# Turning q and k by transposing DMAs instead of TensorE in a streamed two-layer transformer kernel

## The chip, the cores and the metric

The kernel runs on one NeuronCore of one Trainium2 chip. The metric is the device time of one execution in microseconds (us).

## The reference, cut to what matters

The input is two sequences of 2048 tokens of 128 channels. A softmax self-attention comes first, then a two-layer local-attention transformer, then a token-weighting block, then the same two layers again (each behind a layer norm). The change lies wholly in the two-layer block:

```python
def local_attention(q, k, v):                  # 8 heads of 64, windows of 64 tokens
    bq, bk, bv = q.reshape(b, h, w, 64, d) * 8, k.reshape(b, h, w, 64, d), v.reshape(b, h, w, 64, d)
    bk, bv = look_around(bk), look_around(bv)  # the window before, and the own
    sim = einsum('bhwid,bhwjd->bhwij', bq, bk) # masked: i < j or i > j + 64
    return einsum('bhwij,bhwjd->bhwid', softmax(sim), bv)

def _layer(x, ...):
    q, k, v = split(shift_token(x) @ wqkv, 3)
    q, k = rotary_xpos(l2norm(q) * qs, l2norm(k) * ksc)
    x = x + local_attention(q, k, v) @ wo
    h = layernorm(shift_token(x)) @ w1 + b1
    a, g = split(h, 2)
    return x + (a * gelu(g)) @ w2 + b2
```

## The kernel before, in words

Values stay as high and low parts (a value rounded, and the rest), and a product is made of three products of parts (`halves`, L193 to L196). The two-layer block runs twice, as u = 0 and u = 1 (`layers_*`, stages 4 and 8). It streams 128-token tiles: 64 tiles per stage (TS), that is 32 of the first layer and 32 of the second, in STEPS = 68 steps. At step s each engine does its part for several tiles at once: tile s is projected, tile s-1 is normed and gets its rotary factors, tile s-2 is turned, tile s-3 gets its scores, tile s-4 is finished. The feed-forward works on chunks C of 512 tokens (four tiles), spread over the steps by `chunk_at(s, r)`, which is C where s = 4C + r. So the work repeats every four steps.

What each engine does in a step, in the order in which it is written (an engine takes its instructions in that order):

- PE (`layers_pe`): `scores(s-3)` (L647, banks 4 and 5) and `take_off_maxima(s-3)` (L670), `turn(s-2)` (L609: eight fp32 128x128 transposes at L615 from the token rows `ta` into PSUM banks 2 and 3), `turn_result(s-4)` (L696), `project(s)` (L598, q and k into banks 0 and 1), `feed_forward(s)` (L758), `project_out(s-4)` (L703, bank 5), `values(s-2)` (L620, bank 4), `maxima(s-2)` (L628, banks 2 and 3 again), `gather(s-3)` (L679, banks 6 and 7). In the step with `centred` (L738, bank 5) `values` goes ahead of `project_out`.
- ACT (`layers_act`): `exps(s-3)` (L871), `high(s-2)` (L852: the turned q and k out of PSUM, rounded to bf16 into the ring H; L860 copies 64 columns more at the ring's end), `copy_result(s-4)` (L877), `squares(s)` (L840), gates or `square` or `deviation` of the feed-forward, `copy_values(s-2)` (L863), `rnorms(s)` (L845), gelus with two loads of activation tables in every fourth step (L928, L958).
- DVE (`layers_dve`): `divide(s-4)` (L1071), `normed(s-1)` (L1031, which reads banks 0 and 1), `rope(s-1)` (L1040, times cosine into `ta`), `low(s-2)` (L1050: PSUM minus H into the ring L), `gated`, `add_out(s-4)` (L1081), `norms(s)` (L1026), `reduce_maxima(s-2)` (L1064), `scaled` (L1087).
- POOL (`layers_pool`): `rope(s-1)` (L1182: times sine at L1188, two additions into `ta` at L1194), `scale_tables` (L1175), and the low parts of the feed-forward and attention inputs.
- SP (`layers_sp`): issues the DMAs: `tables(s+2)` (L541), shifted inputs (L521), `own(s-2)` (L548) and `past(s-2)` (L555), which copy values across partitions.

Three waits order the neighbours of the change. `project(s)` waits for `normed(s-1)` (L603), as both use banks 0 and 1; `feed_forward(s)` waits for `copy_result(s-4)` (L759 and L760), as bank 7 is used by both; and DVE's `add_out(s-4)` waits for `project_out(s-4)` (L1084) and stands ahead of `norms(s)` and `reduce_maxima(s-2)`.

Of the kernel before, what the change touches and what calls it, by code (L numbers as in the profile page):

```python
# [50 lines left out]
def build(nc, a, out):  # L51
    ctx = ExitStack()
    with ctx:
        def sb(name, shape, dt=F32):
# [10 lines left out]
            "la_pj la_sq la_ss la_rn la_qn la_ta la_tc la_rp la_tr la_hi la_lo la_mx la_mr "  # L65
# [43 lines left out]
        with x_scope:  # L109
# [22 lines left out]
            with ExitStack() as sc:  # L132
                BL = Names(sq=arena(sc, [NH * 2, DH]), qn=arena(sc, [NH * 2, DH]),
                           ta=[arena(sc, [NH * 2, DH]) for _ in range(2)], tc=arena(sc, [NH * 2, DH]),
                           ss=arena(sc, [2, 32]), H=arena(sc, [2, 4, RQ * 128 + 64], BF16),
                           L=arena(sc, [2, 4, RQ * 128 + 64], BF16), mx=[arena(sc, [8], BF16) for _ in range(2)],
                           va=[arena(sc, [NH, DH + 1]) for _ in range(2)], vs=[arena(sc, [NH, DH + 1]) for _ in range(2)],
                           PT=[arena(sc, [2, 512]) for _ in range(2)], rc=[arena(sc, [2, 4, 1]) for _ in range(2)],
                           o=[arena(sc, [2, 4, DH]) for _ in range(2)], ot=[arena(sc, [4, 128]) for _ in range(2)],
                           tb=[arena(sc, [4 * DH]) for _ in range(4)], ysl=arena(sc, [CH]), ysf=arena(sc, [CH]),  # L140
                           hf=[arena(sc, [CH]) for _ in range(2)])
# [374 lines left out]

        def layers_sp(e, stage, u, k):
# [44 lines left out]

            tables(0)
# [4 lines left out]
            for s in range(STEPS):  # L568
                if s + 2 < TS:
                    tables(s + 2)  # L570
                if chunk_at(s, -3):
                    shift_for_attention(chunk_at(s, -3))
                if chunk_at(s, 7) is not None:
                    shift_for_feed_forward(chunk_at(s, 7))
                if 0 <= s - 2 < TS:
                    own(s - 2)
                    past(s - 2)

        def layers_pe(e, stage, u):
# [29 lines left out]
            def turn(i):  # L609
                e.wait_ge(S.la_mr, hi(i))  # L610
                e.wait_ge(S.la_rp, 2 * hi(i) + 2)
                e.wait_ge(S.w_bb, 1)
                for x in range(2):
                    for j in range(4):
                        mm = e.e.transpose(PS[:, 2 + x, j * 128:(j + 1) * 128],  # L615
                                           BL.ta[i % 2][:, 8 * x + 2 * j:8 * x + 2 * j + 2, :].rearrange("p a b -> p (a b)"),
                                           ident)
                mm.then_inc(S.la_tr, 1)
# [84 lines left out]
            def project_out(i):  # L703
# [4 lines left out]
                if chunk_at(i + 4, 9) is not None:  # L708
                    e.wait_ge(S.ff_sq, NC * u + chunk_at(i + 4, 9) + 1)
# [28 lines left out]
            def centred(C):  # L738
                e.wait_ge(S.sf_lo, NC * u + C + 1)
                e.wait_ge(S.la_e, hi(min(4 * C + 6, TS - 1)) + 1)  # L740
                e.e.matmul(PS[:, 5, :], cenr[:, :], fed(HH, C), start=True, stop=False)
                e.e.matmul(PS[:, 5, :], cenr[:, :], fed(HL, C), start=False, stop=True).then_inc(S.ff_cen, 1)
# [15 lines left out]
            def feed_forward(s):  # L758
# [12 lines left out]
                if chunk_at(s, 9) is not None:  # L771
                    centred(chunk_at(s, 9))
# [5 lines left out]
            for s in range(STEPS):  # L778
# [36 lines left out]
            centred(Z)  # L815
# [15 lines left out]
        def layers_act(e, stage, u):  # L831
# [20 lines left out]
            def high(i):  # L852
                c0 = (i % RQ) * 128
                src = PS[:, 2:4, :].rearrange("p x (c q) -> p x c q", q=128)
                e.wait_ge(S.la_tr, hi(i) + 1)
                if i >= RQ - 1:
                    e.wait_ge(S.la_s, hi(i - RQ + 1) + 1)
                o = e.e.copy(BL.H[:, :, :, 64 + c0:192 + c0], src)  # L858
                if i % RQ == RQ - 1 and i % NT < NT - 1:
                    o = e.e.copy(BL.H[:, 1, :, 0:64], src[:, 1, :, 64:128])  # L860
                o.then_inc(S.la_hi, 1)

            def copy_values(i):  # L863
# [5 lines left out]
                e.e.copy(BL.va[i % 2][:, :, 0:DH], PS[:, 4, :].rearrange("p (h d) -> p h d", d=DH)).then_inc(S.la_va, 1)  # L869
# [27 lines left out]
            def square(C):  # L897
# [3 lines left out]
                e.e.activation(BF.sq, PS[:, 5, :], ACT.Square).then_inc(S.ff_sq, 1)  # L901
# [44 lines left out]
            for s in range(STEPS):  # L946
# [49 lines left out]
            square(Z)  # L996
# [11 lines left out]
        def layers_dve(e, stage, u):  # L1008
# [31 lines left out]
            def rope(i):  # L1040
                e.wait_ge(S.la_qn, hi(i) + 1)
                if i >= 2:
                    e.wait_ge(S.la_tr, hi(i - 2) + 1)
                e.wait_ge(S.tb_sc, hi(i) + 1)
                cos = BL.tb[i % 4].rearrange("p (c x o d) -> p c x o d", c=2, x=2, o=1)[:, 0]
                e.e.tensor_tensor(BL.ta[i % 2].rearrange("p (x h) d -> p x h d", x=2),  # L1046
# [69 lines left out]
            for s in range(STEPS):  # L1116
# [55 lines left out]
        def layers_pool(e, stage, u):  # L1172
# [9 lines left out]
            def rope(i):  # L1182
# [9 lines left out]
                tv = BL.ta[i % 2]  # L1192
# [493 lines left out]
```

## Time and profile before

| | us |
|---|---|
| median of 3 runs | 1744.61 (1741.96 to 1745.35) |
| the profiled execution, whole | 1745.16 |
| its span in the profile | 1743.4 |
| first two-layer stage | about 260 to 950 |
| second two-layer stage | about 1020 to 1715 |

| engine | busy | share |
|---|---|---|
| PE (matmul) | 1573.1 | 90% |
| DVE | 1294.5 | 74% |
| ACT | 1190.2 | 68% |
| POOL | 1180.5 | 68% |

The profile shows one execution. Matmuls are pipelined, so their busy times overlap and PE's share is not its share of peak. A chain of waits follows the work that ended last back through what released each piece; a piece's length in that chain is the time it adds, while the mean duration of an instruction in the groups may overlap its neighbours. "to landing" is the time from a DMA's issue to its completion.

### The profile page before, as it was taken

The numbers are of one execution on the slowest core, as the hardware profiler recorded it, in microseconds if no ns is written. First come the engines' busy times: TensorE is split into PE (matmuls) and PEld (weight loads), VectorE is DVE, ScalarE is ACT, GpSimd is POOL, SyncE is SP. The second block draws the span as 40 slices with busy tenths as digits, with TensorE's granted clock in tenths as the row PEclk, the third lists the DMA queues.
The fourth block names the chain that finished last, engine by engine and source line by source line (L and its number), as shares of the span: only waits on it lengthen the run. The fifth ranks groups of instructions, "written<-read, shape, count | busy, mean of one in ns | idle before, by whom it ended". The sixth has DMA issues, their size and how long they took to land.

```text
span 1743.4 us, 47775 instructions
## 1 busy us (share of the span) xinstructions
PE 1573.1 (90%) x20039; PEld 1235.7 (71%) x20039; DVE 1294.5 (74%) x1712; ACT 1190.2 (68%) x1848; POOL 1180.5 (68%) x778
## 2 busy tenths in 40 slices
PE   5999978999999999999986577999999999999986
PEld 4777846877777777777764455877777777777764
DVE  6776657888777877777755867888777877777763
ACT  4886854677766777777765764676776677767764
POOL 3010027888888788888861547888888878888860
PEclk8999988999999999999998887999999999999998
DMA  4000001222222222222110001222222222222111
GB/s 113 25 9 1 0 24 42 66 56 60 51 51 51 62 54 51 51 55 54 42 29 6 1 13 50 66 54 57 56 53 51 53 58 57 50 52 55 45 30 55
DMA packets 66145, 78.87 MB, mean 45 GB/s; under 512 B 14146, under 2 KB 41868, under 8 KB 65932
## 3 DMA queue, kind: packets, MB, share of 16 engines
q1 hardware_dynamic: 65932, 75.82, 17.9%
q8 instruction: 159, 2.61, 0.6%
q14 instruction: 54, 0.44, 0.1%
HBM read 23.10 MB, written 2.10 MB: 14 GB/s over the span
## 4 chain that ended last, share of the span: by engine, by line
PE 60%; ACT 16%; DVE 16%; issue 4%; POOL 2%; DMA 1%; DVEq 0%; POOLq 0%; SPq 0%; ACTq 0%
PE PS L194 9%; PE PS L196 8%; PE PS L195 8%; PE PS L711 7%; PE PS L692 4%; DVE t L1029 4%; PE PS L615 3%; PE PS L667 3%; PE PS L674 2%; ACT t L928 2%; DVE t L1035 2%; ACT L958 2%; ACT t L875 2%; ACT L928 2%; DVE t L1092 2%
## 5 line engine op out<-in xcount | busy, mean ns | idle before, releaser
L1188 POOL TENSOR_TENSOR t<-t 128x1024 f32<-128x1024 f32 x128 | 435.8, 3405 | 101.3 <-DVE t L1035 101.3
L1194 POOL TENSOR_TENSOR t<-t 128x512 f32<-128x512 f32 x256 | 322.1, 1280 | 18.6 <-POOL t L1188 0.4
L1085 DVE TENSOR_TENSOR yT<-PS,yT 128x128 f32<-128x128 f32 x128 | 37.3, 292 | 239.9 <-PE PS L711 239.6
L194 PE MATMUL PS<-wqh,HH 128*128 128x512 f32 x384 | 174.8, 455 | 29.5 <-DVE t L1035 17.9
L875 ACT ACTIVATE t<-PS 128x1024 f32<-128x1024 f32 x128 | 131.3, 1026 | 90.4 <-PE PS L674 89.9
L1212 POOL TENSOR_TENSOR HL<-t,HH 114x512 fp32r<-114x512 f32 (+1 forms) x84 | 118.2, 1421 | 103.9 <-ACT HH L942 103.9
L1046 DVE TENSOR_TENSOR t<-t 128x1024 f32<-128x1024 f32 x128 | 176.7, 1381 | 4.5
L843 ACT ACTIVATE t<-PS 128x1024 f32<-128x1024 f32 x128 | 131.3, 1026 | 71.3 <-PE PS L196 71.2
L1056 DVE TENSOR_TENSOR t<-PS,t 128x1024 bf16<-128x1024 f32 x128 | 155.9, 1218 | 20.7 <-ACT t L860 9.2
L1029 DVE TENSOR_REDUCE t<-t 128x16 f32<-128x1024 f32 x128 | 154.8, 1209 | 17.0 <-ACT t L843 16.7
L711 PEld LDWEIGHTS PS<-t,wo 128*128 128x128 f32 x1024 | 132.0, 192 | 35.4 <-issue 14.4
L1068 DVE TENSOR_REDUCE t<-PS 128x8 bf16<-128x1024 f32 x128 | 155.5, 1215 | 1.2 <-PE PS L641 1.2
L1035 DVE SCALAR_TENSOR_TENSOR t<-t,PS 128x1024 f32<-128x1024 f32 x128 | 154.7, 1209 | 1.9 <-ACT t L850 1.9
L196 PE MATMUL PS<-wqh,HL 128*128 128x512 f32 x384 | 154.9, 403 | 0.0
L195 PE MATMUL PS<-wql,HH 128*128 128x512 f32 x384 | 153.8, 400 | 0.0
L692 PE MATMUL PS<-t 128*64 128x65 f32 x4096 | 147.5, 224 | 0.0
L615 PE MATMUL PS<-cst,t 128*128 128x128 f32 x1024 | 135.5, 276 | 6.6 <-POOL t L1194 6.6
L711 PE MATMUL PS<-t,wo 128*128 128x128 f32 x1024 | 139.1, 279 | 0.4
L692 PEld LDWEIGHTS PS<-t 128*64 128x64 f32 x4096 | 129.8, 137 | 11.8
L858 ACT CAST t<-PS 128x1024 bf16<-128x1024 f32 x128 | 128.0, 1000 | 5.9 <-PE PS L615 5.8
L667 PEld LDWEIGHTS PS<-t 64*128 64x128 bf16 x6144 | 107.3, 95 | 14.3
L615 PEld LDWEIGHTS PS<-cst,t 128*128 128x128 f32 x1024 | 111.4, 142 | 8.3 <-POOL t L1194 8.3
(253 smaller groups left out, 3834.5 us busy)
## 6 DMA issues: line engine op xcount, KB each, us to landing
t<-t SPq DMA_DIRECT2D x254, 130.0 KB, 2.3
t<-in_c_rope SPq DMA_DIRECT2D x128, 128.0 KB, 2.8
t<-yT SPq DMA_DIRECT2D x112, 128.0 KB, 2.4
t<-in_L_attn_a_x SPq DMA_DIRECT2D x4, 512.0 KB, 7.1
out_x<-t SPq DMA_DIRECT2D x8, 256.0 KB, 3.6
t<-yT SPq DMA_DIRECT2D x16, 127.8 KB, 2.3
t<-in_L_ffn_wqkv SPq DMA_DIRECT2D x2, 768.0 KB, 4.2
t<-in_L_ffn_w SPq DMA_DIRECT2D x2, 341.0 KB, 3.3
```

The source lines that it names most:

```text
L194: e.matmul(o, ah, bh, start=not more, stop=False, skip_group_check=True)
L195: e.matmul(o, ah, bl, start=False, stop=False, skip_group_check=True)
L196: return e.matmul(o, al, bh, start=False, stop=stop, skip_group_check=True)
L615: mm = e.e.transpose(PS[:, 2 + x, j * 128:(j + 1) * 128], BL.ta[i % 2][:, 8 * x + 2 * j:8 * x + 2 * j + 2, :].rearrange("p a b -> p (a b)" ...
L692: mm = e.e.matmul(PS[rows[w], 6 + h // 4, 65 * (h % 4):65 * (h % 4) + 65], BL.PT[i % 2][:, h % 2, qs], V[:, h, :], start=True, stop=True, ...
L711: mm = e.e.matmul(PS[:, 5, 0:128], wo[:, l, j, :], BL.ot[i % 2][:, j, :], start=(j == 0), stop=(j == 3))
L875: e.e.activation(BL.PT[i % 2], PS[:, 4:6, :], ACT.Exp).then_inc(S.la_e, 1)
L1029: e.e.tensor_reduce(ss[:, 0:16], BL.sq, AX.X, ALU.add).then_inc(S.la_ss, 1)
L1035: e.e.scalar_tensor_tensor(BL.qn, ss[:, 16:32].rearrange("p (a o) -> p a o", o=1) .to_broadcast([128, 2 * NH, DH]), 1e12, PS[:, 0:2, :].re ...
L1046: e.e.tensor_tensor(BL.ta[i % 2].rearrange("p (x h) d -> p x h d", x=2), BL.qn.rearrange("p (x h) d -> p x h d", x=2), cos.to_broadcast([1 ...
L1188: e.e.tensor_tensor(BL.tc.rearrange("p (x h) d -> p x h d", x=2), BL.qn.rearrange("p (x h) d -> p x h d", x=2), sin.to_broadcast([128, 2, ...
L1194: e.e.tensor_tensor(tv[:, :, 32 * s:32 * s + 32], tv[:, :, 32 * s:32 * s + 32], BL.tc[:, :, 32 * (1 - s):32 * (1 - s) + 32], ALU.add).then ...
```

## The change

q and k no longer go through PSUM on their way to head-by-head layout. ACT's `high` rounds the token rows `ta` to bf16 (`qh`), DVE's `low` takes the rest as bf16 (`ql`), both from SBUF, and SP issues one transposing DMA of 128x1024 bf16 for each into the rings H and L, and a second, smaller one for each at the ring's end (every fourth tile, the last tile of a sequence apart). `ta` has one buffer in place of two. Banks 2 to 5 are dealt out anew: `values` uses bank 2 and stands ahead of `project`; `centred` uses bank 3. The semaphore la_tr goes, la_ht and la_lt come.

```diff
+        def turned(u, i):
+            return 16 * ((TS + TS // RQ - TS // NT) * u + i + i // RQ - i // NT)
...
 layers_sp
+            def turn(i, part, to, ready, sem):
+                c0 = (i % RQ) * 128
+                e.wait_ge(ready, hi(i) + 1)
+                if i >= RQ - 1:
+                    e.wait_ge(S.la_s, hi(i - RQ + 1) + 1)
+                e.wait_ge(sem, turned(u, i))
+                e.e.dma_start(to[:, :, :, 64 + c0:192 + c0].rearrange("p x c q -> p (x c) q"), part,
+                              transpose=True).then_inc(sem, 16)
+                if i % RQ == RQ - 1 and i % NT < NT - 1:
+                    e.e.dma_start(to[:, 1, :, 0:64], part[64:128, NH * DH:], transpose=True).then_inc(sem, 16)
...
                 if s + 2 < TS:
                     tables(s + 2)
+                if 0 <= s - 2 < TS:
+                    turn(s - 2, BL.qh, BL.H, S.la_hi, S.la_ht)
+                    own(s - 2)
+                    turn(s - 2, BL.ql, BL.L, S.la_lo, S.la_lt)
...
                 if 0 <= s - 2 < TS:
-                    own(s - 2)
                     past(s - 2)
...
 layers_pe
-            def turn(i):
-                e.wait_ge(S.la_mr, hi(i))
-                e.wait_ge(S.la_rp, 2 * hi(i) + 2)
-                e.wait_ge(S.w_bb, 1)
-                for x in range(2):
-                    for j in range(4):
-                        mm = e.e.transpose(PS[:, 2 + x, j * 128:(j + 1) * 128],
...
             def values(i):
-                e.wait_ge(S.la_e, hi(i))
+                e.wait_ge(S.la_mr, hi(i))
-                halves(e.e, PS[:, 4, :], h, hl, wqh[:, l, 1024:1536], wql[:, l, 1024:1536]).then_inc(S.la_v, 1)
+                halves(e.e, PS[:, 2, :], h, hl, wqh[:, l, 1024:1536], wql[:, l, 1024:1536]).then_inc(S.la_v, 1)
             def maxima(i):
-                e.wait_ge(S.la_hi, hi(i) + 1)
-                e.wait_ge(S.la_lo, hi(i) + 1)
+                e.wait_ge(S.la_ht, turned(u, i + 1))
+                e.wait_ge(S.la_lo, hi(i))
                 e.wait_ge(S.la_k0, u + 1)
+                e.wait_ge(S.la_va, hi(i) + 1)
+                e.wait_ge(S.w_bb, 1)
+                if chunk_at(i + 2, 9) is not None:
+                    e.wait_ge(S.ff_sq, NC * u + chunk_at(i + 2, 9) + 1)
             def scores(i):
-                e.wait_ge(S.la_va, hi(i) + 1)
+                e.wait_ge(S.la_e, hi(i))
                 e.wait_ge(S.la_out, hi(i - 1))
-                e.wait_ge(S.la_lo, hi(i) + 1)
+                e.wait_ge(S.la_lt, turned(u, i + 1))
             def centred(C, bank):
-                e.wait_ge(S.la_e, hi(min(4 * C + 6, TS - 1)) + 1)
+                e.wait_ge(S.la_mr, hi(min(4 * C + 6, TS - 1)) + 1)
...
                 if on(3):
                     scores(s - 3)
                     take_off_maxima(s - 3)
-                if on(2):
-                    turn(s - 2)
                 if on(4):
                     turn_result(s - 4)
+                if on(2):
+                    values(s - 2)
                 if on(0):
                     project(s)
                 feed_forward(s)
-                late = chunk_at(s, 9) is not None
-                if on(4) and not late:
-                    project_out(s - 4)
-                if on(2):
-                    values(s - 2)
-                if on(4) and late:
+                if on(4):
                     project_out(s - 4)
                 if on(2):
                     maxima(s - 2)
...
 layers_act
             def high(i):
+                e.wait_ge(S.la_rp, 2 * hi(i) + 2)
+                e.wait_ge(S.la_ht, turned(u, i))
+                e.wait_ge(S.la_lo, hi(i))
+                e.e.copy(BL.qh, BL.ta.rearrange("p a b -> p (a b)")).then_inc(S.la_hi, 1)
...
-                if on(3) and not after_gelus:
-                    exps(s - 3)
                 if on(2):
                     high(s - 2)
+                if after_gelus:
+                    e.e.preload_act_table_set("natural_log_exp_and_others")
+                if on(3):
+                    exps(s - 3)
                 if on(4):
                     copy_result(s - 4)
-                if after_gelus:
-                    e.e.preload_act_table_set("natural_log_exp_and_others")
-                if on(3) and after_gelus:
-                    exps(s - 3)
+                if on(2):
+                    copy_values(s - 2)
                 if on(0):
                     squares(s)
...
 layers_dve
             def rope(i):
                 e.wait_ge(S.la_qn, hi(i) + 1)
-                if i >= 2:
-                    e.wait_ge(S.la_tr, hi(i - 2) + 1)
+                e.wait_ge(S.la_lo, hi(i))
             def low(i):
                 e.wait_ge(S.la_hi, hi(i) + 1)
+                e.wait_ge(S.la_lt, turned(u, i))
+                o = e.e.tensor_tensor(BL.ql, BL.ta.rearrange("p a b -> p (a b)"), BL.qh, ALU.subtract)
...
                 if on(1):
                     normed(s - 1)
-                    rope(s - 1)
                 if on(2):
                     low(s - 2)
+                if on(1):
+                    rope(s - 1)
```

## Rows read from the trace of the kernel before

**Rows 1.** The page's part 1: busy us (share of the span) xinstructions.

```profile
PE 1573.1 (90%) x20039; PEld 1235.7 (71%) x20039; DVE 1294.5 (74%) x1712; ACT 1190.2 (68%) x1848; POOL 1180.5 (68%) x778
```

**Rows 2.** Windows: length, then busy us (xcount) by engine, PE clock, DMA share, GB/s.

```profile
300.00:900.00 600.00, 575.85 (x8759) 458.62 (x8757) 475.67 (x565) 426.71 (x666) 508.41 (x326) 1.00 0.22 53
900.00:960.00 60.00, 42.82 (x274) 28.93 (x274) 30.86 (x47) 33.82 (x52) 14.90 (x11) 0.86 0.03 7
```

**Rows 3.** The same view, one cycle of four steps, cut at `add_out`.

```profile
502.94:512.58 9.64, 9.18 (x146) 7.50 (x145) 8.15 (x10) 7.71 (x13) 9.50 (x7) 1.00 0.18 45
512.58:522.96 10.38, 10.38 (x152) 8.57 (x151) 6.93 (x9) 5.75 (x9) 9.94 (x7) 1.00 0.28 65
522.96:535.33 12.37, 11.09 (x154) 8.09 (x156) 9.31 (x12) 10.10 (x15) 8.88 (x7) 1.00 0.23 55
535.33:544.05 8.72, 8.70 (x142) 7.06 (x140) 7.92 (x10) 5.86 (x10) 5.98 (x4) 1.00 0.20 47
```

**Rows 4.** Chain of waits in that cycle, second step: start us, us, engine, line.

```profile
511.65 0.89 PE PS L711 x8
512.54 0.23 PE PS L194
...
513.24 0.34 PE PS L636 x4
...
513.80 1.08 PE PS L692 x32
...
516.46 0.88 PE PS L615 x8
...
517.77 0.23 PE PS L194
```

**Rows 5.** Timeline: start us, us, engine, line, operation, shapes, idle before it.

```profile
502.81 2.53 POOL L1194 TENSOR_TENSOR t<-t 128x512 f32<-128x512 f32 x2
...
507.34 1.21 DVE L1035 SCALAR_TENSOR_TENSOR t<-t,PS 128x1024 f32<-128x1024 f32 x1
...
512.58 0.29 DVE L1085 TENSOR_TENSOR yT<-PS,yT 128x128 f32<-128x128 f32 x1 [1.42 <-PE PS L711]
...
515.88 1.21 DVE L1035 SCALAR_TENSOR_TENSOR t<-t,PS 128x1024 f32<-128x1024 f32 x1
...
538.64 1.21 DVE L1035 SCALAR_TENSOR_TENSOR t<-t,PS 128x1024 f32<-128x1024 f32 x1
```

**Rows 6.** Chain of waits, third step: table load and exponentials.

```profile
530.28 1.28 ACT L958
531.58 1.03 ACT t L875
```

**Rows 7.** Groups of instructions: line, engine, operation, shapes | busy us, mean ns | idle before.

```profile
L1046 DVE TENSOR_TENSOR t<-t 128x1024 f32<-128x1024 f32 x128 | 176.7, 1381 | 4.5
L1056 DVE TENSOR_TENSOR t<-PS,t 128x1024 bf16<-128x1024 f32 x128 | 155.9, 1218 | 20.7 <-ACT t L860 9.2 <-ACT t L858 7.4
...
L858 ACT CAST t<-PS 128x1024 bf16<-128x1024 f32 x128 | 128.0, 1000 | 5.9 <-PE PS L615 5.8
...
L881 ACT COPY t<-PS 128x512 f32<-128x512 f32 x128 | 76.9, 600 | 1.9 <-PE PS L700 1.9
...
L860 ACT CAST t<-PS 128x256 bf16<-128x256 f32 x24 | 9.0, 375 | 0.0
```

**Rows 8.** DMA queues and issues: out<-in, KB each, median us to landing.

```profile
q1 hardware_dynamic: 65932, 75.82, 17.9%
...
t<-t SPq DMA_DIRECT2D x254, 130.0 KB, 2.3
...
t<-in_L_attn_a_x SPq DMA_DIRECT2D x4, 512.0 KB, 7.1
out_x<-t SPq DMA_DIRECT2D x8, 256.0 KB, 3.6
...
t<-cstv SPq DMA_DIRECT2D x16, 0.2 KB, 2.0
```

More of the change, by code:

```diff
@@ L64, in build @@
             "tb_ld tb_sc ys_l sl_hi sl_lo ys_f sf_hi sf_lo "
-            "la_pj la_sq la_ss la_rn la_qn la_ta la_tc la_rp la_tr la_hi la_lo la_mx la_mr "
+            "la_pj la_sq la_ss la_rn la_qn la_ta la_tc la_rp la_hi la_lo la_ht la_lt la_mx la_mr "
             "la_v la_va la_own la_past la_s la_e la_d la_rc la_ot la_ox la_oe la_po la_out la_k0 "
@@ L133, in build @@
                 BL = Names(sq=arena(sc, [NH * 2, DH]), qn=arena(sc, [NH * 2, DH]),
-                           ta=[arena(sc, [NH * 2, DH]) for _ in range(2)], tc=arena(sc, [NH * 2, DH]),
+                           ta=arena(sc, [NH * 2, DH]), qh=arena(sc, [2 * NH * DH], BF16), ql=arena(sc, [2 * NH * DH], BF16),
+                           tc=arena(sc, [NH * 2, DH]),
                            ss=arena(sc, [2, 32]), H=arena(sc, [2, 4, RQ * 128 + 64], BF16),
@@ L707, in project_out @@
                 e.wait_ge(S.la_out, hi(i))
-                if chunk_at(i + 4, 9) is not None:
-                    e.wait_ge(S.ff_sq, NC * u + chunk_at(i + 4, 9) + 1)
                 for j in range(4):
@@ L736, in first, with centred @@
                 halves(e.e, PS[0:CW[i], bank, :], w1h[:, l, cs], w1l[:, l, cs], fed(HH, C), fed(HL, C)).then_inc(sem, 1)
-            def centred(C):
+            def centred(C, bank):
                 e.wait_ge(S.sf_lo, NC * u + C + 1)
-                e.wait_ge(S.la_e, hi(min(4 * C + 6, TS - 1)) + 1)
-                e.e.matmul(PS[:, 5, :], cenr[:, :], fed(HH, C), start=True, stop=False)
-                e.e.matmul(PS[:, 5, :], cenr[:, :], fed(HL, C), start=False, stop=True).then_inc(S.ff_cen, 1)
+                e.wait_ge(S.la_mr, hi(min(4 * C + 6, TS - 1)) + 1)
+                e.e.matmul(PS[:, bank, :], cenr[:, :], fed(HH, C), start=True, stop=False)
+                e.e.matmul(PS[:, bank, :], cenr[:, :], fed(HL, C), start=False, stop=True).then_inc(S.ff_cen, 1)
             def variance(C, bank):
@@ L771, in feed_forward @@
                 if chunk_at(s, 9) is not None:
-                    centred(chunk_at(s, 9))
+                    centred(chunk_at(s, 9), 3)
                 if chunk_at(s, 14) is not None:
@@ L814, in layers_pe @@
             e.wait_ge(S.la_out, last)
-            centred(Z)
+            centred(Z, 5)
             e.wait_ge(S.la_e, last)
@@ L852, in high @@
             def high(i):
[L853 to L861, printed above, removed]
+                e.wait_ge(S.la_rp, 2 * hi(i) + 2)
+                e.wait_ge(S.la_ht, turned(u, i))
+                e.wait_ge(S.la_lo, hi(i))
+                e.e.copy(BL.qh, BL.ta.rearrange("p a b -> p (a b)")).then_inc(S.la_hi, 1)
             def copy_values(i):
@@ L868, in copy_values @@
                     e.wait_ge(S.la_past, 16 * (hi(i - 2) + 1 - u))
-                e.e.copy(BL.va[i % 2][:, :, 0:DH], PS[:, 4, :].rearrange("p (h d) -> p h d", d=DH)).then_inc(S.la_va, 1)
+                e.e.copy(BL.va[i % 2][:, :, 0:DH], PS[:, 2, :].rearrange("p (h d) -> p h d", d=DH)).then_inc(S.la_va, 1)
             def exps(i):
@@ L895, in high_for_feed_forward, with square @@
                 e.e.copy(fed(HH, C), BL.ysf).then_inc(S.sf_hi, 1)
-            def square(C):
+            def square(C, bank):
                 G = NC * u + C
@@ L900, in square @@
                 e.wait_ge(S.ff_var, G)
-                e.e.activation(BF.sq, PS[:, 5, :], ACT.Square).then_inc(S.ff_sq, 1)
+                e.e.activation(BF.sq, PS[:, bank, :], ACT.Square).then_inc(S.ff_sq, 1)
             def deviation(C, bank):
@@ L970, in layers_act @@
                 if chunk_at(s, 9) is not None:
-                    square(chunk_at(s, 9))
+                    square(chunk_at(s, 9), 3)
                 if chunk_at(s, 10) is not None:
                     deviation(chunk_at(s, 10), 7)
-                if on(2):
-                    copy_values(s - 2)
                 if on(0):
@@ L995, in layers_act @@
             high_hidden(B, 1)
-            square(Z)
+            square(Z, 5)
             high_hidden(B, 2)
@@ L1191, in rope @@
                 e.wait_ge(S.la_tc, g + 1)
-                tv = BL.ta[i % 2]
+                tv = BL.ta
                 for s in range(2):
```

13 lines of the change are left out of this document (2 added, 11 removed).

## The prediction

> **What bounds the kernel now.** I read the busy shares first: PE's 90% stands far above the rest [rows 1], and through the stream it is busy 576 of 600 us at the full clock, 2.4 GHz [rows 2]. That invites "less work on PE, less time". So I cut one four-step cycle into its steps at `add_out` [rows 3] and read the chain of waits and the timeline in it. I call the steps A, B, C, D: A is s mod 4 = 3, B is 0, C is 1, D is 2. Their lengths are 9.64, 10.38, 12.37 and 8.72 us, 41.1 together.
>
> From one `project_out` to the next `project` two paths run side by side. On PE, A to B: from 512.54 to 517.77 us, 5.23 us, with `turn` as 0.88 of it [rows 4]. On DVE: `add_out`, `norms`, `reduce_maxima`, `divide`, `normed`, from 512.58 to 515.88 + 1.21 = 517.09 us, 4.5 us [rows 5]; `project` may not start before. So PE is late by only about 0.6 us. From C to D `normed` ends at 538.64 + 1.21 = 539.85 us, 4.5 us after `add_out` at 535.33 [rows 3, 5], and `project` starts there at 539.9: a tie. From D to A DVE also has `scaled`, its `normed` ends at 508.55 us, 5.6 us after 502.94 [rows 3, 5], and PE waits for it. In C the chain leaves PE for ACT: gelus, `high`, L860, `copy_result`, table load, `exps` [rows 6, 7].
>
> **The change, part by part.**
>
> *PE's turning goes.* Eight transposes, 0.88 us of the chain in a tile [rows 4]; over 128 tiles 113 us, if PE were the bound everywhere. New PE path from `project_out` to `project`: 5.23 - 0.88 = 4.35 us (`values` has only moved inside it). DVE's path takes 4.5, and no edit shortens it. So the gain at A to B is what PE was late, about 0.4 us after the 0.1 us of handing over; at C to D none; at D to A none; at B to C none, as ACT's chain takes over there.
>
> *ACT in step C.* Before, from the end of `high` to `centred`: L860, `copy_result`, load, `exps`. ACT's instructions overlap by a tenth of a us, so in the chain high adds 0.9, L860 0.3, copy_result 0.5 and the load and exps 1.28 and 1.03 [rows 6, 7]: 4.0 us to 532.6, and 2.7 more to the step's end at 535.3 [rows 3], 6.7 together; the gelus end at 528.6. Now `copy_result` follows `exps`, and `feed_forward` waits for it: high 0.9, load 1.28, exps 1.03, copy_result 0.6, 3.8 us, then six matmuls of `first` at 0.23 each, 1.4, `centred` some 0.7, `project_out` 0.9 [rows 4]: 6.8 to 6.9 us. A loss of 0.2 us. A cycle so has -0.4 + 0.2 = -0.2 us if all else is hidden.
>
> *ACT's high and DVE's low from SBUF.* `high` 1.0 us as before; `low` 1.22 from PSUM, and 1.38 is what an SBUF operation of that size takes beside POOL [rows 7]. Bounds -0.2 and +0.4 us; I take +0.16. It hides in DVE's wait for `project_out`, 1.4 us ahead of L1085 at 512.58 [rows 5]. With that wait gone it would cost its 0.16.
>
> *One buffer of ta.* DVE's `rope(s-1)` now waits for `low(s-2)`, which waits for `high(s-2)`, which waits for POOL's additions; those end at 502.81 + 2.53 = 505.34 us, 3 us before `normed` ends [rows 5]. I take nothing. Were POOL 3 us later, `low` and `rope` would wait behind it with `add_out` queued after them. L860 goes, 0.37 us of ACT in the ring's last tile, counted above.
>
> *The transposing DMAs.* Two per tile, 256 KB each, and two smaller every fourth tile, on SP's queue, where `own`, `past`, `tables` and the shifts wait behind them. No row shows a transposing DMA. Bounds for its time to landing, T: 256 KB stored plainly takes 3.6 us, and below it lies the 2.3 us of 130 KB; above, 1024 pieces at the queue's mean packet time. That is 0.179 x 16 x 1743.4 / 65932 = 76 ns, so 1024 x 76 ns / 16 = 4.8 us beside a fixed 2.0, 6.9 us [rows 8]. A 128x1024 bf16 tile read in runs of 128 elements is 1024 pieces; the output of 256 KB leaves in 512 runs of 512 bytes and takes 3.6 us, 1.6 above the 2.0 us of a tiny copy. By pieces then T = 2.0 + 2 x 1.6 = 5.2 us; the 512 KB loads, 1024 such runs, took 7.1 us in company [rows 8]. I take 5.2, as I expect pieces to count and not bytes, and keep 2.3 and 6.9.
>
> What is due when (new times in the cycle's clock, from the sums above). *The high part*: A, `high` ends at 508.3 us, behind `normed` of the layer norm, and `maxima` now follows `project_out` directly, 512.6: room 4.3 us. D has 4.2, B and C over 5. *The low part*: its DMA stands behind `own`, which waits for `copy_values`, on ACT behind exps and copy_result. In A `copy_values` ends at 510.5, `own` is issued by 511.0; `scores` want it after maxima and gather, 0.56 + 1.08 us [rows 4] past 512.6, so at 514.2: room 3.2 us, and 0.2 of PE's slack. In C copy_values ends at 533.1, the issue is at 533.6, scores come at 535.6 + 1.64 = 537.2: room 3.6, slack 0.2, and here a second transfer follows, 256 more pieces, 0.8 us. In D room 3.6 and slack 1.3 (DVE's `scaled`). In B there is over 5 us, since step C waits for ACT anyway.
>
> With T = 5.2: A 5.2 - 3.2 - 0.2 = 1.8; C 5.2 + 0.8 - 3.6 - 0.2 = 2.2; D 5.2 - 3.6 - 1.3 = 0.3; B 0. Together 4.3, less 0.2, is +4.1 us a cycle. Two stages have 16 cycles each, of which I count 14 as full: 28 x 4.1 = +115 us. In the fill of each stage the first two tiles wait in the open for T in place of 0.88: 4 x 4.3 = +17 us. The sum is +132 on the profiled execution's 1745.2, 1877 us; the median shown is 0.6 us lower, which is nothing here.
>
> With PE waiting more, its clock may fall: it was 0.86 where PE was busy 71% [rows 2]. Here it would be busy (39.3 - 2.1) / 45.3 = 82%. At 0.93 the PE part of a cycle, some 25 us, costs 1.8 more, 50 us in all. I leave it out of the point and in the range.
>
> **The rivals.**
>
> *It lands like a plain copy* (T between 2.3 and 3.6). For: all bytes move inside SBUF, and a plain copy there lands in 2.3 us. Against: nothing but that. At 3.6: A 0.2, C 0.6, less 0.2: 0.6 x 28 + 4 x 2.7 = +28, 1773 us; at 2.3 the cycles give 6 us back and the fills take 6, 1745. Chance 0.25. The Trainium skill, "Advanced Engine Details and Errata", X-Bar Transpose (TRN2), says that transposing DMAs are as fast as regular ones, and "DMA: Bandwidth & Descriptors", Latency and other measured facts, gives 261 GB/s for one kernel; the estimate from these pages is 1.0 us over a fixed 2.0, and this rival. No row here bears them out or not.
>
> *Faster* (chance 0.07). If DVE's path is not the floor that I read, both `turn`s in the cycle's chain and L860 go: 2 x 0.88 + 0.27 us, times 28, 57 us less, 1688 us. It decides where `normed` ends before PE reaches `project`; for it speaks that PE is at 96% in the stream; against it the tie at 539.9 and that `normed` is waited for at 508.55. It needs T under 3.4 as well.
>
> *The DMA engines become the bound* (0.25). If a transposing DMA holds them 4.8 us (76 ns per piece), two hold them 9.6 us of a step of 10.3, on top of the 22% that they are busy now [rows 2], 2.3 us: 11.9 us a step, 1.6 x 128 = +205 us, 1950. T is 6.9 then, by the sum above A 3.5, C 3.9, D 2.0, less 0.2: 28 x 9.2 + 4 x 6.0 = +282, 2027, and I take that, as the later end. With pieces of 32 bytes, which nothing here excludes, it would be a multiple. The Trainium skill, "VectorE: DVE Perf Modes", The three transpose paths, sets 1309 ns for a 128x128 block by DMA against 390 ns by TensorE; eight in turn would be an estimate of 10.5 us for a tile, this rival and worse. The trace has 0.88 / 8 = 0.11 us a block on TensorE in the chain.
>
> *It isn't a crossbar transfer at all*, but element by element: thousands of us more. Chance 0.03.
>
> The forecast has 0.40. From no change a measurement here can tell about 0.2%, 3.5 us. Faster: 0.07 and 0.03 of the plain-copy case, 0.10. Same: 0.06 of that case. Slower: the rest, 0.84. The range goes from 1744 (plain copy) to 2110 (engines bound, or forecast with a lower clock and T = 6.9); outside are 0.10 below and about 0.1 above.
>
> **What would show it.** L615 gone, PE idle between `gather` and L656/L667 with "DMA t<-t" as releaser, 1 to 2 us in A and C and nearly none in B; cycles of about 45 us; landing of the transposes near 5 us; DVE's path from L1085 to the end of L1035 still 4.5 us. Wrong: landing under 3.5 us and cycles of 41 (then the first rival), cycles near 39 (the second), PE waiting on the high part's DMA at L636 and a DMA share over 0.8 (the third).

## The result and the profile after

| | us |
|---|---|
| before, median of 4 runs of this comparison | 1743.3 |
| after, median of 4 runs | 1841.0 |
| ratio, with its 95% interval | 1.0556 (1.053 to 1.0581) |
| the profiled execution after, whole / span | 1840.6 / 1838.8 |

The change costs 97.7 us. The forecast was slower, +132 us, in a range from 1744 to 2110 us. The page's part 1 of the kernel after, and its windows over the stream (columns as in [rows 2]) and over one cycle, cut at `add_out` in the order C, D, A, B:

```profile
PE 1506.3 (82%) x19015; PEld 1179.1 (64%) x19015; DVE 1502.0 (82%) x1688; ACT 1174.6 (64%) x1824; POOL 1144.6 (62%) x778
```

```profile
300.00:900.00 600.00, 507.12 (x7785) 403.24 (x7785) 536.58 (x518) 389.12 (x608) 460.16 (x306) 0.97 0.52 103
...
502.99:516.84 13.85, 10.51 (x143) 8.14 (x144) 9.97 (x12) 9.22 (x13) 9.06 (x8) 0.89 0.38 78
516.84:526.92 10.08, 9.18 (x156) 6.89 (x156) 9.96 (x9) 6.72 (x11) 6.33 (x4) 0.98 0.56 120
526.92:536.87 9.95, 8.62 (x145) 6.99 (x147) 9.82 (x10) 7.18 (x12) 8.95 (x6) 1.00 0.44 94
536.87:547.10 10.23, 9.33 (x131) 7.44 (x129) 9.08 (x10) 5.68 (x9) 8.91 (x6) 1.00 0.55 117
```

PE fell from 90% to 82%, as its work went, and DVE rose from 74% to 82% [rows 1], though it has no instruction more. In steps D and A it is busy 9.96 of 10.08 and 9.82 of 9.95 us, with the time included in which an instruction stands and waits for POOL: there DVE is the bound now. The groups of instructions tell where its 207 us came from (POOL's multiplication, POOL's additions, `rope`, `low`; for the last two compare [rows 7]):

```profile
L1184 POOL TENSOR_TENSOR t<-t 128x1024 f32<-128x1024 f32 x128 | 402.7, 3146 | 69.2 <-DVE t L1035 68.7
L1190 POOL TENSOR_TENSOR t<-t 128x512 f32<-128x512 f32 x256 | 319.4, 1269 | 183.9 <-DVE t L1045 183.6
L1045 DVE TENSOR_TENSOR t<-t 128x1024 f32<-128x1024 f32 x128 | 356.3, 2784 | 11.5
L1052 DVE TENSOR_TENSOR t<-t 128x1024 bf16<-128x1024 f32 x128 | 207.5, 1621 | 39.1 <-ACT t L863 39.0
```

The same multiplication by the cosine took 1381 ns and takes 2784; `low` went from 1218 to 1621 ns. The timeline of step D shows how:

```profile
520.14 1.21 DVE L1035 SCALAR_TENSOR_TENSOR t<-t,PS 128x1024 f32<-128x1024 f32 x1
...
521.27 1.75 DVE L1052 TENSOR_TENSOR t<-t 128x1024 bf16<-128x1024 f32 x1
...
521.90 3.35 POOL L1184 TENSOR_TENSOR t<-t 128x1024 f32<-128x1024 f32 x1
...
523.11 3.22 DVE L1045 TENSOR_TENSOR t<-t 128x1024 f32<-128x1024 f32 x1
...
526.92 0.27 DVE L1080 TENSOR_TENSOR yT<-PS,yT 128x128 f32<-128x128 f32 x1
```

POOL's multiplication ends at 525.25 us, and `rope`, begun at 523.11, ends 1.1 us after that: it stood until POOL was done and then took its own 1.2 us. `low` began at 521.27 inside another POOL operation (L1208, to 521.94), took 1.75 and ended 1.1 us after that one. The wait that DVE had ahead of `add_out` [rows 5] is gone at the end of D and of A (0.7 and 1.4 us before); at the end of B and C one of about 1 and 0.6 to 1.8 us is left.

DMAs and their landing, and PE's waits for them in the whole run:

```profile
q1 hardware_dynamic: 350092, 146.11, 39.5%
...
t<-t SPq DMA_TRANSPOSE x304, 3.2
```

```profile
PE PS L670 <- DMA t<-t: 39.3, 25, 2.9
PE PS L650 <- DMA t<-t: 8.1, 8, 3.0
```

A transposing DMA lands in 3.2 us, not 5.2, and PE waits for them some 47 us in all, in 33 waits (the last two numbers of a line are the count and the longest, us). About 26 of these are in the first twelve tiles of the two stages, and only 14 in the cycles behind them. The packets cost little: (0.395 x 1838.8 - 0.179 x 1743.4) x 16 / (350092 - 65932) = 23 ns each, where I had taken 76 for the upper bound [rows 8].

In step C the timeline and the windows show something else (ACT's high, load, exps, copy_result; PE; then the window of what PE does next):

```profile
508.55 1.03 ACT L863 CAST t<-t 128x1024 bf16<-128x1024 f32 x1
...
509.59 1.28 ACT L956 ACT_TABLE_LOAD   x1
...
510.89 1.02 ACT L877 ACTIVATE t<-PS 128x1024 f32<-128x1024 f32 x1
...
511.81 0.58 ACT L883 COPY t<-PS 128x512 f32<-128x512 f32 x1
...
512.44 0.50 PE L195 MATMUL PS<-HH,w1h 128*114 128x512 f32 x1 [2.56 <-ACT t L883]
...
514.89 1.91 PE L723 MATMUL PS<-t,wo 128*128 128x128 f32 x8
```

```profile
512.44:516.84 4.40, 4.40 (x20) 3.60 (x24) 2.09 (x4) 1.97 (x3) 3.20 (x3) 0.65 0.56 112
512.44:514.04 1.60, 1.60 (x7) 1.22 (x7) 1.18 (x2) 1.37 (x2) 0.94 (x1) 0.92 0.12 22
514.04:516.84 2.80, 2.80 (x15) 2.38 (x17) 0.91 (x3) 0.60 (x1) 2.26 (x3) 0.50 0.81 164
```

In the same place the kernel before has two short waits, and its `project_out` takes 1.16 us:

```profile
530.32 0.49 PE L194 MATMUL PS<-HH,w1h 128*114 128x512 f32 x1 [0.48 <-ACT t L881]
...
532.75 0.47 PE L741 MATMUL PS<-HH,cenr 128*128 128x512 f32 x1 [0.78 <-ACT t L875]
...
534.13 1.16 PE L711 MATMUL PS<-t,wo 128*128 128x128 f32 x8
```

ACT takes 3.8 us from the start of `high` to the end of `copy_result`, as I had summed, and PE stands 2.56 us in one piece. Over the 4.4 us behind it the granted clock is 0.65 in the mean: 0.92 while the six matmuls of `first` run, then 0.50, which is the lower level, 1.2 GHz, for `centred` and `project_out`, whose eight matmuls take 1.91 us instead of 1.16.

The same wait of 2.56 us did not always bring this. In the first stage, from the 12th tile on, the clock fell in 10 of 12 steps C, which then took 13.7 to 14.1 us; in the other two it stayed at 1.00, 2.4 GHz, and they took 12.5 us, against 12.1 to 12.4 before. One of these two:

```profile
546.92:559.38 12.46, 9.11 (x143) 7.04 (x143) 9.90 (x11) 9.21 (x13) 8.19 (x7) 1.00 0.33 71
```

With both stages it is 21 of 24. So at the full clock the change lengthens C by only 0.1 to 0.4 us, and the lower clock adds 1.5 where it comes: an estimate of 21 x 1.5 = 32 us of the 97.7. What decides whether it falls after one and the same wait, the runs do not show.

From the start of `add_out` of every tile I took the mean length of each step from the 12th tile of the first two-layer stage on (13 intervals for each; the last C, at the stage's end, is a short one of 9.6 us after and 11.4 before), beside the time of the tiles before and of the whole stage, in us. The kernels e4 to e12 are told below:

```
                         A      B      C      D    cycle  first 12  stage
before                  9.35  10.37  12.23   8.62   40.6    95.6   623.2
after                   9.78   9.95  13.42   9.92   43.1   106.7   666.7
e5  low from SBUF       9.68   9.99  12.24   9.90   41.8   105.6   649.0
e12 copy_result early   9.64   9.96  11.13  10.65   41.4   105.2   643.0
e9  low, one input      8.98  10.04  13.10   9.19   41.3   108.1   645.2
e11 the same, plain     9.12  10.19  12.59   9.04   40.9   103.1   635.3
e4  extra transpose     9.85  10.70  13.24  10.37   44.2   119.8   693.8
e8  norms first         9.92  10.38  11.56   8.40   40.3    94.5   618.1
```

The two profiled executions lie 95.4 us apart. The stage is 43.5 us longer, the second one 43.3; the other 9 us lie ahead of each stage's first tile and at the ends. Of the 43.5, 11 are in the first twelve tiles and the rest in the cycles: C +1.2, D +1.3, A +0.4, B -0.4.

### The profile page after: what moved, and what is told of

Its sections match the earlier page's. It is cut to its first block and busy times, and to the rows that moved or that the text cites. A ratio compares the mean times of both kernels' runs of the same rounds, so it can differ in the third digit from the quotient of the medians.

```text
span 1838.8 us, 46496 instructions
## 1 busy us (share of the span) xinstructions
PE 1506.3 (82%) x19015; PEld 1179.1 (64%) x19015; DVE 1502.0 (82%) x1688; ACT 1174.6 (64%) x1824; POOL 1144.6 (62%) x778
## 2 busy tenths in 40 slices
DMA packets 350303, 149.08 MB, mean 81 GB/s; under 512 B 298306, under 2 KB 326028, under 8 KB 350092
## 3 DMA queue, kind: packets, MB, share of 16 engines
q1 hardware_dynamic: 350092, 146.11, 39.5%
## 5 line engine op out<-in xcount | busy, mean ns | idle before, releaser
L1184 POOL TENSOR_TENSOR t<-t 128x1024 f32<-128x1024 f32 x128 | 402.7, 3146 | 69.2 <-DVE t L1035 68.7
L1045 DVE TENSOR_TENSOR t<-t 128x1024 f32<-128x1024 f32 x128 | 356.3, 2784 | 11.5
L1052 DVE TENSOR_TENSOR t<-t 128x1024 bf16<-128x1024 f32 x128 | 207.5, 1621 | 39.1 <-ACT t L863 39.0
L855 ACT ACTIVATE t<-t,cstv 128x16 f32<-128x16 f32 x128 | 39.4, 308 | 275.1 <-DVE t L1029 275.1
L195 PE MATMUL PS<-wqh,HH 128*128 128x512 f32 x384 | 172.2, 448 | 21.9 <-DVE t L1035 12.4
L1208 POOL TENSOR_TENSOR HL<-t,HH 114x512 fp32r<-114x512 f32 (+1 forms) x84 | 118.2, 1421 | 100.8 <-ACT HH L944 100.8
L723 PEld LDWEIGHTS PS<-t,wo 128*128 128x128 f32 x1024 | 150.9, 212 | 26.0 <-issue 14.4
L195 PE MATMUL PS<-HH,w1h 128*114 128x512 f32 (+1 forms) x192 | 84.2, 439 | 82.5 <-ACT t L883 72.2
L723 PE MATMUL PS<-t,wo 128*128 128x128 f32 x1024 | 149.5, 294 | 0.0
L863 ACT CAST t<-t 128x1024 bf16<-128x1024 f32 x128 | 133.1, 1040 | 25.3 <-POOL t L1190 25.2
L436 DVE TENSOR_TENSOR t<-t 128x1024 fp32r<-128x1024 f32 x64 | 78.2, 1224 | 52.6 <-ACT t L411 52.3
L681 PEld LDWEIGHTS PS<-t 64*128 64x128 bf16 x6144 | 111.0, 96 | 14.6 <-issue 0.7
```

The source lines that it names most:

```text
L195: e.matmul(o, ah, bh, start=not more, stop=False, skip_group_check=True)
L723: mm = e.e.matmul(PS[:, 5, 0:128], wo[:, l, j, :], BL.ot[i % 2][:, j, :], start=(j == 0), stop=(j == 3))
L1045: e.e.tensor_tensor(BL.ta.rearrange("p (x h) d -> p x h d", x=2), BL.qn.rearrange("p (x h) d -> p x h d", x=2), cos.to_broadcast([128, 2, ...
L1052: o = e.e.tensor_tensor(BL.ql, BL.ta.rearrange("p a b -> p (a b)"), BL.qh, ALU.subtract)
L1184: e.e.tensor_tensor(BL.tc.rearrange("p (x h) d -> p x h d", x=2), BL.qn.rearrange("p (x h) d -> p x h d", x=2), sin.to_broadcast([128, 2, ...
```

## The experiments

Each was timed in 3 rounds (e12 in 5) against the kernel before on the same chip; ratios are to it. The kernel before had medians of 1742.0 to 1743.4 us in these sets, so that a difference between kernels of two sets is good to a few us. I began with two theories: P, that DVE's `rope` meets POOL's multiplication because `low` now stands ahead of it; and L, my forecast, that PE waits for the landings.

**e1.** POOL waits for DVE's rope.

```diff
 layers_pool, rope
+                e.wait_ge(S.la_ta, g + 1)
                 sin = BL.tb[i % 4]...
```

> The changed kernel with one wait more: POOL starts its sine multiplication (L1184 of the changed kernel) only when DVE's rope (L1045) is done. Theory P (order of the two): DVE's rope takes 3.2 us instead of 1.2 because it is started while POOL's sine multiplication runs and stands still until that ends. Then here L1045 takes 1.2 to 1.4 us in the median, POOL's additions start about when they did, and the time falls by at least half of the 97.7 us lost, to 1745-1790 us. Theory L (landing, my forecast's mechanism): PE waits for the transposing DMAs; nothing of them is changed here, so the time stays at 1830-1850 us.

Measured: 1857.9 us, 1.0661 (1.0639 to 1.0683). The three groups:

```profile
L1185 POOL TENSOR_TENSOR t<-t 128x1024 f32<-128x1024 f32 x128 | 304.1, 2376 | 377.7 <-DVE t L1045 377.7
L1052 DVE TENSOR_TENSOR t<-t 128x1024 bf16<-128x1024 f32 x128 | 210.0, 1640 | 56.5 <-ACT t L863 54.0
L1045 DVE TENSOR_TENSOR t<-t 128x1024 f32<-128x1024 f32 x128 | 179.1, 1399 | 11.5
```

`rope` is short again, as P had it, and the time isn't: 17 us more than the change, above both ranges. POOL now stands 378 us for `rope`, and with one buffer of ta the ring rope, multiplication, additions, high, low is walked through in turn. Moving the wait to the other engine mends nothing.

**e2.** Two buffers of ta, rope ahead of low.

```diff
 layers_dve
                 if on(1):
                     normed(s - 1)
+                    rope(s - 1)
                 if on(2):
                     low(s - 2)
-                if on(1):
-                    rope(s - 1)
```

> The changed kernel with two buffers of ta and DVE's rope(s-1) ahead of low(s-2), as before the change (hf moved to free space). Theory P: rope starts with POOL's multiplication again, not behind it; L1045 at 1.2-1.5 us, time 1735-1770 us. Theory L: the transposing DMAs are as they were, 1830-1850 us.

Measured: 1882.6 us, 1.0799 (1.0776 to 1.0822). P fell here: 42 us slower than the change, and above both ranges.

```profile
L1188 POOL TENSOR_TENSOR t<-t 128x1024 f32<-128x1024 f32 x128 | 434.4, 3394 | 139.5 <-DVE t L1040 139.5
L1057 DVE TENSOR_TENSOR t<-t 128x1024 bf16<-128x1024 f32 x128 | 424.2, 3314 | 6.0 <-ACT t L868 6.0
L1194 POOL TENSOR_TENSOR t<-t 128x512 f32<-128x512 f32 x256 | 421.1, 1664 | 18.6 <-POOL t L1188 0.4
```

Now `low` comes behind `rope`, begins within POOL's multiplication and takes 3.3 us; POOL's additions wait for it in turn (1664 ns for 1280 before).

**e3.** The kernel before, with low ahead of rope (the edit of e2 the other way round).

> The kernel before with one edit: DVE does low(s-2) ahead of rope(s-1). No transposing DMA at all. Theory P: rope now starts in the middle of POOL's sine multiplication, takes about 3.2 us, and most of the loss of the change appears: 1800-1845 us. Theory L: 1740-1750 us, no change.

Measured: 1751.3 us, 1.0044 (1.0028 to 1.006). The order alone costs 8 us: `rope` grew to 1650 ns in the mean, but DVE's wait ahead of `add_out` took that in. P is a small part.

**e4.** One more transposing DMA, ahead of each low part's.

```diff
 layers_sp
+                    e.wait_ge(S.la_lo, hi(s - 2) + 1)
+                    e.wait_ge(S.la_dm, 16 * hi(s - 2))
+                    e.e.dma_start(BL.dm, BL.ql, transpose=True).then_inc(S.la_dm, 16)
                     turn(s - 2, BL.ql, BL.L, S.la_lo, S.la_lt)
```

> The changed kernel with one more 128x1024 transposing DMA (of the same data, to a tile that nobody reads) issued ahead of each low part's. The low part lands 1.3 us or more later. Theory L: PE's waits for it grow by 1.3-3 us in two of four steps, +60 to +170 us. Theory P: DVE's chain covers it, under +20 us.

Measured: 1892.4 us, 1.0856 (1.0793 to 1.0919), 51 us over the change. PE's waits:

```profile
PE PS L678 <- DMA t<-t: 143.6, 79, 4.2
```

By the table 13 of the 27 us in a stage are in the first twelve tiles, and the cycle is 1.1 us longer, in B and D. So the change stands near the edge: its landings are mostly covered, and another 1.3 us of issue are not. That is between the theories.

P being too narrow, I formed S: DVE and POOL exclude each other whenever a DVE operation has two SBUF inputs. `low` had one and a PSUM input; now it has two, in whatever order.

**e5.** The kernel before, only low's inputs both from SBUF.

```diff
 layers_dve, low
-                o = e.e.tensor_tensor(BL.L[...], src, BL.H[...], ALU.subtract)
+                ta = BL.ta[i % 2].rearrange("p (x c a) d -> p x c (a d)", x=2, c=4)
+                o = e.e.scalar_tensor_tensor(BL.L[...], ta, 0.0, BL.H[...], ALU.mult, ALU.mult)
```

> The kernel before, its turning on TensorE and its order of work kept; only DVE's low takes both inputs from SBUF: (ta times 0) times H in place of PSUM minus H, the same 1024 columns, so that L is zero and the low parts of q and k are left out of the scores. Theory S (DVE and POOL exclude each other while a DVE operation has two SBUF inputs; low moved from PSUM to SBUF puts 1.2 us a tile more under that exclusion): low takes well over 1.22 us (1.6 to 3.3), POOL's operations lengthen, and much of the change's loss appears without any transposing DMA: 1775-1860 us. Theory L (PE waits for the landing of the DMAs): 1738-1750 us.

Measured: 1798.4 us, 1.0321 (1.0302 to 1.034): +56 us without any transposing DMA. The group, and one step of the timeline:

```profile
L1057 DVE SCALAR_TENSOR_TENSOR t<-t 128x1024 bf16<-128x1024 f32 x128 | 417.1, 3258 | 16.9 <-ACT t L860 8.4 <-ACT t L858 7.6
```

```profile
524.07 3.39 POOL L1190 TENSOR_TENSOR t<-t 128x1024 f32<-128x1024 f32 x1
...
525.14 3.41 DVE L1057 SCALAR_TENSOR_TENSOR t<-t 128x1024 bf16<-128x1024 f32 x1
...
527.60 3.29 POOL L1196 TENSOR_TENSOR t<-t 128x512 f32<-128x512 f32 x2
...
528.47 0.28 DVE L1087 TENSOR_TENSOR yT<-PS,yT 128x128 f32<-128x128 f32 x1
```

POOL's multiplication ends at 527.46, `low` 1.1 us later, and POOL's additions (2.5 us alone) wait for `low` meanwhile. In the table e5 has the steps A, B and D of the changed kernel to 0.1 us, and its first twelve tiles nearly so; only C is that of before. Its operation isn't a longer one by itself: the shortest of the 128 took 1.22 us, and the median 3.39. This settles what lengthens A and D.

**e6, e7.** The changed kernel, and e2, with low's work done by one input.

```diff
 layers_dve, low
-                o = e.e.tensor_tensor(BL.ql, BL.ta..., BL.qh, ALU.subtract)
+                e.e.tensor_reduce(BL.rd, BL.ta, AX.X, ALU.add)
+                o = e.e.tensor_tensor(BL.ql[:, 0:8], BL.qh[:, 0:8], BL.qh[:, 0:8], ALU.subtract)
```

> The changed kernel, its DMAs and order kept; DVE's low is replaced by a reduction of ta (one SBUF input, 1.2 us as well) and a subtraction of 8 columns, so that the low parts of q and k are zero. Theory S: low no longer contends with POOL; most of the loss goes, 1745-1790 us. Theory L: DMAs and their issue times unchanged, 1825-1845 us.

> The same replacement of low in the changed kernel with two buffers of ta and rope ahead of low (1883 us before it). Theory S: 1740-1780 us, as rope starts with POOL's multiplication and low doesn't contend. Theory L: 1860-1890 us.

Measured: e6 1799.6 us, 1.0325 (1.029 to 1.036); e7 1835.9 us, 1.0548 (1.052 to 1.0575). Both short of S, and the timeline of e6 shows a fault of mine:

```profile
518.45 2.40 POOL L1186 TENSOR_TENSOR t<-t 128x1024 f32<-128x1024 f32 x1
...
518.92 1.94 DVE L1053 TENSOR_TENSOR t<-t 128x8 bf16<-128x8 bf16 x1
```

The subtraction of 8 columns has two SBUF inputs as well and stood until POOL was done at 520.85: 1.94 us for 8 columns. The exclusion hangs on the operands, not on the amount of data.

**e9, e10.** The same with a memset of the 8 columns (`e.e.memset(BL.ql[:, 0:8], 0.0)`).

> As e6, but the 8 columns are set by a memset instead of a subtraction: in e6 that subtraction of 8 columns, with two SBUF inputs, took 1.5 to 1.9 us, as it stood until POOL's multiplication ended. Now nothing of low contends; the low parts of q and k are zero. Theory S: the 1.7 us come off DVE's chain; L1045 (rope) then starts inside POOL's multiplication and waits in its place, so the gain is partial: 1760-1800 us. Theory L: what e6 left over (+57 us) is PE waiting for landings, so it stays at 1790-1805 us.

> As e7 (two buffers of ta, rope ahead of low), with the memset in place of the subtraction of 8 columns. Here no DVE operation waits for POOL but those that did before the change. Theory S alone: 1740-1755 us, as the kernel before. Theory L for the rest: low's end comes later in the step than in the new order, its DMA lands late for scores, and 1770-1835 us remain with PE's waits on DMA at L675 over 30 us in 300 to 900.

Measured: e9 1785.5 us, 1.0226 (1.0192 to 1.026); e10 1786.5 us, 1.0239 (1.0218 to 1.026). With low's second SBUF input gone the change is 55 us faster, much like the 56 that e5 added to the kernel before; against e2 it is 96. In e9 `rope` still stands for POOL (2246 ns in the mean), but in e10 it takes 1368 ns, as in the kernel before, and 43 us remain: those aren't S. By the table C keeps its 13.1 us in e9, with the 2.6 us wait of PE in it and a lowered clock in 10 of 24 steps; PE's waits for landings are 53 us for L670. In e10 they are 26 us for L675 in 300 to 900, just short of the 30 that I had asked of L.

**e11.** e9 with plain copies of the same bytes in place of the transposing DMAs.

```diff
 layers_sp, turn
-                e.e.dma_start(to[...].rearrange("p x c q -> p (x c) q"), part, transpose=True)...
+                e.e.dma_start(to[...].rearrange("p x c q -> p (x c) q"), part.rearrange("p (a q) -> p a q", q=128))...
 layers_act, high
-                e.e.copy(BL.qh, ...)
+                e.e.activation(BL.qh, ..., ACT.Square, scale=0.0)
```

> e9 with plain DMAs of the same bytes in place of the transposing ones, and high writing zeros (times 0.0), so that q and k are left out of the scores. A plain one is issued in about 0.5 us instead of 1.25 and lands in 2.3 to 2.6 us instead of 3.0 to 3.2. Theory L: with the high and low parts there about 1.5 us earlier, PE's DMA waits go and the time falls by 20-50 us against e9. Theory S, or ACT's order and single buffer being the rest: within 10 us of e9.

q and k are left out here, so that this run tells of time alone. Measured: 1758.7 us, 1.0086 (1.0059 to 1.0113), 27 us under e9; the profiled execution, of which the table tells, took 11 us more than this median. The landing is hardly sooner:

```profile
t<-t SPq DMA_DIRECT2D x256, 256.0 KB, 3.0
```

What differs more is SP's time to issue one: 0.63 us plain (median of L576 in this run), 1.30 us transposing (the same line in the changed kernel), two a tile. So some 27 us hang on issue and landing together in e9; which of the two it is was not parted.

**e12.** The changed kernel, copy_result ahead of the table load in step C.

```diff
 layers_act
+                if on(4) and after_gelus:
+                    copy_result(s - 4)
                 if after_gelus:
                     e.e.preload_act_table_set("natural_log_exp_and_others")
                 if on(3):
                     exps(s - 3)
-                if on(4):
+                if on(4) and not after_gelus:
                     copy_result(s - 4)
```

> The changed kernel with one thing of its ACT order undone: in the step after the gelus, copy_result(s-4) stands ahead of the table load and exps, as before the change. Theory A (ACT's order in step C): in the changed kernel PE waits there 2.6 us in one piece for copy_result and then runs at a granted clock of 0.65 for 4.4 us, so that the step is some 1.5 us longer than before; undone, PE's waits for L883 go, the clock stays at 1.00, and the time falls by 20-45 us, to 1795-1820 us. Against it: DVE's chain with low and rope covers the step, and the time falls by less than 10 us.

Measured: 1784.7 us, 1.0251 (1.0226 to 1.0276): 56 us back, more than the 20 to 45 expected. Step C in the timeline, and a window over it:

```profile
503.15 0.58 ACT L883 COPY t<-PS 128x512 f32<-128x512 f32 x1
...
503.74 1.28 ACT L958 ACT_TABLE_LOAD   x1
...
503.78 0.49 PE L195 MATMUL PS<-HH,w1h 128*114 128x512 f32 x1 [0.23 <-ACT t L883]
...
506.12 1.16 PE L723 MATMUL PS<-t,wo 128*128 128x128 f32 x8 [0.25 <-ACT t L877]
```

```profile
502.00:508.00 6.00, 4.79 (x23) 3.25 (x22) 4.64 (x5) 5.92 (x8) 3.52 (x2) 1.00 0.35 69
```

The one wait of 2.56 us became 0.23 and 0.25, the clock stays at 1.00, 2.4 GHz, in every step C, and C takes 11.1 us. That is 1.1 us less than before the change, so the 56 us are more than what ACT's order had cost. 0.7 us of it reappear in D: most steps D take 10.1 us, as in the change, but three took 12.1 to 12.8 at a granted clock of 0.86 or 0.87. PE's waits for L670 rise to 74 us: the landings come into the open as C shortens.

**e8.** The kernel before, norms ahead of add_out.

```diff
 layers_dve
+                if on(0):
+                    norms(s)
                 if on(4):
                     add_out(s - 4)
                 if chunk_at(s, 16) is not None:
                     add_second(chunk_at(s, 16), 7)
-                if on(0):
-                    norms(s)
```

> The kernel before with norms(s) ahead of add_out(s-4) and add_second on DVE. My step that DVE's path from project_out to project (add_out, norms, reduce_maxima, divide, normed) is the floor of three steps: with norms ahead of the wait for project_out that path is 1.2 us shorter, and the gelus of step C start earlier. If so, 1685-1730 us. If PE's work alone bounds the steps, 1738-1750 us.

Measured: 1732.3 us, 0.994 (0.9924 to 0.9956). It is faster than both kernels, but by 10 us and not by the 12 to 57 that DVE's path being the floor would give, nor by the 4 at most of the other theory: C and D got shorter (11.56 and 8.40 us), A longer (9.92). So the step of the prediction that made this path the floor of three steps is borne out in part at best.

## Why the prediction was right, and where it was not

**The sign and the size** held: slower, 97.7 us of a forecast 132, inside the range. That they did is luck. The sum was nearly all landing, 4.3 us a cycle; with the T that was measured it gives 28 x (0.2 - 0.2) + 4 x 2.3 = +9 us, almost no change. The 97.7 us came mainly from two places that the sum had priced at 0 and at 0.2 us a cycle. The prediction's own sign of being wrong, a landing under 3.5 us, came true, though its cycle of 41 us did not: it was 43.1.

**The landing.** T was taken as 5.2 us and is 3.2. The step that failed is the one that priced pieces at 3.1 ns (1.6 us for 512): 256 KB in 1024 pieces landed in 3.2 us transposed and in 3.0 plain (e11), no later than the 3.6 of the output's 512 runs [rows 8]. With 3.2 my own sum has no lateness in A and D, and 0.2 in C; PE's waits for landings are 14 us in the cycles of the run, where I had 4.3 us a cycle, 120 in all. The Trainium skill's statement that transposing DMAs are as fast as regular ones ("Advanced Engine Details and Errata", X-Bar Transpose (TRN2)) agrees in the landing, 3.2 against 3.0 us in e11. SP's issue, 1.30 against 0.63 us, is another matter, and I had no term for it. The rival "lands like a plain copy" was right on T and gave 1745 to 1773 us, since it shared the next step with the forecast.

**high and low from SBUF** was the other step that failed, and the dearer one. I bounded `low` by -0.2 and +0.4 us from L1046's 1381 ns, "beside POOL", and covered it by DVE's wait. But that mean came from an operation that starts just ahead of POOL's (0.05 to 0.5 us in the cycle of [rows 3]); started behind it, an operation with two SBUF inputs ends 1.1 us after POOL's. `low` and `rope` together grew by 0.4 + 1.4 us a tile, the cover was 0.7 to 1.4 us in A and D, and the step priced at 0 costs 56 us (e5, and e9 from the other side). The Trainium skill has the rule in "SBUF — State Buffer", Who interferes with whom: a DVE instruction with two SBUF inputs contends with a GpSimd instruction that reads SBUF, and the later one is held until the first ends. The trace agrees: DVE's end lies 1.1 us behind POOL's in e5 and in the change, its own duration being 1.2.

**One buffer of ta** at nothing: the order that it forces costs 8 us in the kernel before (e3), and e10, with two buffers and the old order, is no faster than e9. That was near.

**ACT in step C.** I had the edit, its place and its 3.8 us, and priced the PE work behind it at the rows' 0.23 us a matmul and 0.9 for `project_out`. Where the clock stayed full that was right: those steps take 12.5 us. But in 21 of 24 steps it fell, and C costs 1.2 us in the mean, not 0.2. I had looked for the fall of the clock in PE's share over a cycle and left it out of the point (the 82% there takes 2.1 us of work off PE's cycle, where 4 x 0.88 = 3.5 give 79%; no other number rests on it). It came behind one wait of 2.6 us where there had been two of 0.5 and 0.8, and with that wait gone (e12) it stayed at 1.00 in C. Undoing the order gives back 56 us in all, since C then also becomes shorter than it was before the change.

**The gain at A to B** was forecast at 0.4 us (by its own 0.6 and 0.1 it is 0.5) and B is 0.4 us shorter, but e5 has the same B with all its turning on TensorE. So the number is no evidence that TensorE's 0.88 us were worth anything; what shortens B when A and D grow was not tried.

**What adds up.** Undoing low's contention gives 55 us, undoing ACT's order 56, plain copies 27 of what the first leaves: 138, more than the 97.7. So they are not shares of it; e12 gives more than the order had cost, and that each covers a part of the others is argued, not shown. Both main ones undone at once were not tried, nor what makes the first twelve tiles 10 us longer in e5, e9 and e12 alike.

## What to carry to other kernels

Moving an operand from PSUM to SBUF is not free on DVE where POOL is busy: count the SBUF inputs of each DVE operation, and read the mean of a contended one together with who started first. When an engine's order is changed, look at the longest single wait that PE is left with and at the granted clock behind it, not only at the sum of the waits. When a forecast comes true, put the measured sizes into its sum before believing its mechanism. Taking work from the busiest engine (PE at 90%) brought no gain that a run here shows.

## What the runs showed of the hardware

- A DVE subtraction of 8 columns with two SBUF inputs took 1.94 us beside a POOL operation (median 1.47 us over 128, 0.15 at the least).
- A 128x1024 bf16 transposing DMA within SBUF occupies SP for 1.30 us (median) and lands in 3.0 to 5.2 us, median 3.2; the plain one of the same bytes occupies it for 0.63 us and lands in 3.0 (median). A packet added by the change costs 23 ns of one DMA engine in the mean.
- Behind a PE wait of 2.56 us in step C the granted clock fell to 0.50 (1.2 GHz) in 21 of 24 steps of the change and stayed at 1.00 in three; the step took 13.7 to 14.1 us with the fall and 12.5 without. Behind waits of 0.48 and 0.78 us (before) and of 0.23 and 0.25 us (e12) it stayed at 1.00 in step C.
- Beside a POOL multiplication, DVE's `low` with one SBUF and one PSUM input took 1218 ns in the mean, and with both from SBUF 3258 (e5).
